# A mixer and FFN kernel: x1 transposed by DMA in f16 halves instead of by TensorE, and 1/den spread over the channels by DMA instead of by a matmul

## The reference, cut to what matters

```python
for _ in range(2):                       # two levels of analysis filters (4 taps, every second token)
    h = dwconv(low, g_filter)[:, ::2]; low = dwconv(low, h_filter)[:, ::2]
q = elu(h16) + 1.0                       # h16: low in 16 heads of 32 channels; k = q, v = h16
kv = einsum('bnhd,bnhe->bhde', q, v);  z = q.sum(axis=1)
num = einsum('bnhd,bhde->bnhe', q, kv)
den = einsum('bnhd,bhd->bnh', q, z)[..., None] + 1e-6
low = num / den
for h in reversed(highs):                # two levels of synthesis filters on doubled tokens
    low = dwconv(repeat(low, 2), h_synth) + dwconv(repeat(h, 2), g_synth)
x1 = _layernorm(x + layer_norm(x + low, gamma, beta))
out = _layernorm(x1 + (silu(x1 @ wg.T) * (x1 @ wu.T)) @ wd.T)
```

## Time and profile before

| | us |
|---|---|
| median of three runs | 1384.56 |
| profiled execution, span from first to last instruction | 1382.5 |
| median above the span | 2.1 |
| TensorE busy | 1245.5 (90%) |
| VectorE busy | 988.1 (71%) |
| ScalarE busy | 688.8 (50%) |
| GpSimd busy | 373.0 (27%) |
| iterations 1 to 8, from first `gate_up` to first `gate_up` | 155.6, 154.1, 154.4, 148.0, 144.4, 144.4, 144.3, 127.6 |

### The profile page before, as it was taken

How to read it: one execution, slowest core, us unless ns; L and a number is a source line. 1 busy time by engine, 2 the same in 40 slices (tenths; PEclk the granted TensorE clock), 3 DMA queues, 4 the chain that set the end, 5 groups by cost and what they waited for, 6 DMA issues and landing times.

```text
span 1382.5 us, 18903 instructions
## 1 busy us (share of the span) xinstructions
PE 1245.5 (90%) x5920; PEld 629.5 (46%) x5920; DVE 988.1 (71%) x1913; ACT 688.8 (50%) x1384; POOL 373.0 (27%) x790
## 2 busy tenths in 40 slices
PE   3997039998999989998999999999999999999998
PEld 3885025444444444444544444444444444444443
DVE  2677938988688958988489738883898478854332
ACT  2663046345753466346753466346634664365432
POOL 2001033133423044223413143304321341234101
PEclk9998559999999999999999999999999999999999
DMA  8963033000520014000500041002200130010000
GB/s 262 285 238 123 0 123 108 23 24 24 176 77 31 0 55 147 20 23 24 176 16 31 8 148 30 31 1 84 100 23 8 53 122 23 15 38 24 16 16 31
DMA packets 48465, 95.20 MB, mean 69 GB/s; under 512 B 8448, under 2 KB 25088, under 8 KB 47376
## 3 DMA queue, kind: packets, MB, share of 16 engines
q1 hardware_dynamic: 48400, 94.42, 20.8%
HBM read 69.21 MB, written 25.19 MB: 68 GB/s over the span
## 4 chain that ended last, share of the span: by engine, by line
DVE 29%; PE 27%; issue 22%; ACT 12%; POOL 9%; SPq 0%; DMA 0%; DVEq 0%; POOLq 0%; ACTq 0%
DVE s_chan L864 6%; DVE h_f L1070 5%; DVE low L864 5%; PE ps_down L540 3%; PE ps_down L539 3%; PE ps_gate L522 3%; PE ps_gate L523 3%; PE ps_up L523 3%; PE ps_up L522 3%; DVE hid L1076 3%; POOL rs L819 3%; DVE h_mem L864 3%; PE ps_down L572 2%; ACT junk L671 2%; DVE l L864 2%
## 5 line engine op out<-in xcount | busy, mean ns | idle before, releaser
L522 PE MATMUL ps_gate<-x_hi,w 128*128 128x512 f16 x768 | 292.4, 381 | 27.5 <-DVE h_f L1070 25.4
L539 PE MATMUL ps_down<-w,hid 128*128 128x512 f16 x768 | 292.1, 380 | 0.1
L540 PE MATMUL ps_down<-w,hid 128*128 128x512 f16 x768 | 292.1, 380 | 0.0
L523 PE MATMUL ps_gate<-x_lo,w 128*128 128x512 f16 x768 | 292.0, 380 | 0.0
L522 PE MATMUL ps_up<-x_hi,w 128*128 128x512 f16 x768 | 291.1, 379 | 0.0
L523 PE MATMUL ps_up<-x_lo,w 128*128 128x512 f16 x768 | 291.1, 379 | 0.0
L758 ACT ACTIVATE hid<-h_f 128x512 f16<-128x512 f32 x192 | 121.0, 630 | 203.2 <-DVE h_f L1070 203.2
L1070 DVE SCALAR_TENSOR_TENSOR h_f<-ps_up,gate_s 128x512 f32<-128x512 f32 x192 | 131.7, 686 | 123.7 <-ACT gate_s L754 123.1
L1076 DVE TENSOR_TENSOR hid<-h_f,hid 128x512 f16<-128x512 f32 x192 | 139.3, 725 | 57.7 <-ACT hid L758 56.8
L754 ACT ACTIVATE gate_s<-ps_gate 128x512 f32<-128x512 f32 x192 | 112.1, 584 | 70.0 <-PE ps_up L523 69.8
L522 PEld LDWEIGHTS ps_gate<-x_hi,w 128*128 128x128 f16 x768 | 75.2, 98 | 124.9 <-DVE h_f L1070 42.2
(11 more groups left out here) (106 smaller groups left out, 1803.8 us busy)
## 6 DMA issues: line engine op xcount, KB each, us to landing
xa<-x_chan SPq DMA_DIRECT2D x32, 515.0 KB, 5.6
xb<-x_chan SPq DMA_DIRECT2D x8, 2060.0 KB, 8.9
xt<-x_tok SPq DMA_DIRECT2D x64, 256.0 KB, 2.6
out<-z SPq DMA_DIRECT2D x64, 256.0 KB, 2.0
hid<-weights SPq DMA_DIRECT2D x12, 768.0 KB, 6.7
q_in<-q_scratch SPq DMA_DIRECT2D x8, 518.0 KB, 8.5
h_in<-h_scratch SPq DMA_DIRECT2D x8, 518.0 KB, 9.5
h_scratch<-h SPq DMA_DIRECT2D x8, 512.0 KB, 9.2
```

The source lines that it names most:

```text
L522: pe.matmul(ps_gu[k % 2][g][:, :], w, x1_hi[:, b, c, :], start=(c == 0), stop=False)
L523: mm = pe.matmul(ps_gu[k % 2][g][:, :], w, x1_lo[:, b, c, :], start=False, stop=(c == NC - 1))
L539: pe.matmul(ps_d[t % 2][:, :], h_hi[:, k, t * P:(t + 1) * P], w, start=(k == 0), stop=False)
L540: mm = pe.matmul(ps_d[t % 2][:, :], h_lo[:, k, t * P:(t + 1) * P], w, start=False, stop=(k == NH - 1))
```

## The change

x1 is split in token layout. ScalarE writes the f16 high half from the same inputs as x1 just before x1 itself (one more pass in `normx`), GpSimd subtracts it from x1 for the low half (a new `normx` there), and SyncE transposes both halves by DMA, two DMAs per tile (`norm3` on SyncE). The halves of a tile lie in the tile's own buffer of `xt` (`x1_tok`), so `xt` is loaded again only after both transposes have landed (`reload`). TensorE's `norm3`, ScalarE's copy and VectorE's subtraction are gone. The first `gate_up` of a block waits for eight landings.

The sums of den go to four groups of 32 columns, one per 128 channels, each a matmul of its own; den then has 128 partitions, 4 useful ones in each group of 32. SyncE stores 1/den to DRAM, waits for that, and loads it four times, each row repeated over the 32 channels of its head, straight into `att`, which now has four buffers. The spreading matmul and its copy are gone.

```diff
@@ BESIDE: block 0 of an iteration, then block 1 @@
-    (0, 4): [(LATE, "kv", 0), (LATE, "blocks", 0), (NOW, "norm3", 4), (NOW, "xbeta", 7), (NEXT, "high1", 0)],
+    (0, 4): [(LATE, "kv", 0), (LATE, "blocks", 0), (NOW, "norm3", 5), (NOW, "reload", 4), (NOW, "xbeta", 6),
+             (NEXT, "high1", 0)],
...
-    (1, 13): [(NEXT, "norm3", 0), (NEXT, "normx", 2), (NEXT, "norm2", 3), (NEXT, "normq", 3)],
-    (1, 14): [(NEXT, "norm3", 1), (NEXT, "normx", 3)],
-    (1, 15): [(NEXT, "norm3", 2)],
-    (1, 15.5): [(NEXT, "norm3", 3), (ANA, "exp", 0)],
+    (1, 13): [(NEXT, "norm3", 1), (NEXT, "reload", 0), (NEXT, "normx", 2), (NEXT, "norm2", 3), (NEXT, "normq", 3)],
+    (1, 14): [(NEXT, "norm3", 2), (NEXT, "reload", 1), (NEXT, "normx", 3)],
+    (1, 15): [(NEXT, "reload", 2), (NEXT, "norm3", 3), (NEXT, "reload", 3)],
+    (1, 15.5): [(ANA, "exp", 0)],
...
+    den_dram = nc.dram_tensor("den_scratch", [P, QW], F32, kind="Internal").ap()
...
-        z_heads = sb("z_heads", [P, NC, HEADS])
-        den = sb("den", [HEADS, QW])
-        att = sb("att", [P, 2, QW])
+        z_heads = sb("z_heads", [P, NC, HEAD])
+        den = sb("den", [P, QW])
+        att = sb("att", [P, NC, QW])
+        x1_tok = xt[:, :, :].rearrange("p t c -> p (t c)").bitcast(F16).rearrange("p (t w c) -> p t w c", t=4, w=2)
...
@@ SyncE @@
-            def after_norm2(j, batch, t):
+            def norm3(j, batch, t):
+                b, u = t // DSUB, t % DSUB
+                if not first(j):
+                    hold(sp, gu_ready, NH * (2 * j + b - 1))
+                for w, (x1_part, ready) in enumerate(((x1_hi, x1_hi_ready), (x1_lo, x1_lo_ready))):
+                    hold(sp, ready, SUBS * j + t + 1)
+                    sp.dma_start_transpose(x1_part[:, b, :, u * P:(u + 1) * P], x1_tok[:, u, w, :]
+                                           ).then_inc(x1_turned[w][u], 16)
+
+            def reload(j, batch, t):
...
-                hold(sp, r_ready, SUBS * j + t + 1)
+                for w in range(2):
+                    hold(sp, x1_turned[w][t % DSUB], 16 * (2 * j + t // DSUB + 1))
                 load_xt(j + (t + 4) // SUBS, (t + 4) % SUBS)
+
+            def dens(j, batch, _):
+                hold(sp, den_step, 2 * (j + 1))
+                sp.dma_start(den_dram[:, :], den[:, :]).then_inc(st_den, 16)
+                hold(sp, st_den, 16 * (j + 1))
+                for c in range(NC):
+                    rows = den_dram[c * HEAD:c * HEAD + CHUNK_HEADS, :]
+                    sp.dma_start(att[:, c, :], rows[:, None, :].to_broadcast([CHUNK_HEADS, HEAD, QW])
+                                 ).then_inc(ld_att[c], 16)
...
@@ TensorE @@
             def dens(j, batch, _):
...
-                    mm = pe.matmul(ps_y[0:HEADS, 0:QW], z_heads[:, c, :], q_in[:, c, :], start=(c == 0),
-                                   stop=(c == NC - 1))
+                    mm = pe.matmul(ps_y[c * HEAD:(c + 1) * HEAD, 0:QW], z_heads[:, c, :], q_in[:, c, :],
+                                   start=True, stop=True)
...
             def attend(j, batch, c):
...
-                pe.matmul(ps_y[:, 0:QW], spread[:, c, :], den[:, :], start=True, stop=True)
                 pe.matmul(ps_x[:, 0:QW], kv_blocks[:, c, :], q_in[:, c, :], start=True, stop=True
                           ).then_inc(qk_ready, 1)
...
-            def norm3(j, batch, t):
...
-                for c in range(NC):
-                    mm = pe.transpose(ps_y[:, c * P:(c + 1) * P], x1[:, t, c * P:(c + 1) * P], ident[:, :])
-                mm.then_inc(x1_turned, 1)
...
             def gate_up(B, b, k):
                 if k == 0:
-                    pe.wait_ge(x1_hi_ready, DSUB * (B + 1))
-                    pe.wait_ge(x1_lo_ready, DSUB * (B + 1))
+                    for u in range(DSUB):
+                        pe.wait_ge(x1_turned[0][u], 16 * (B + 1))
+                        pe.wait_ge(x1_turned[1][u], 16 * (B + 1))
...
@@ ScalarE @@
-            def attend(j, batch, c):
...
-                nc.scalar.activation(att[:, c % 2, :], ps_y[:, 0:QW], ACT.Copy).then_inc(rden_out, 1)
...
             def normx(j, batch, t):
...
+                nc.scalar.activation(x1_tok[:, t % DSUB, 0, :], x1[:, t, :], ACT.Identity, bias=rs2[:, t, 5:6],
+                                     scale=rs2[:, t, 4:5]).then_inc(x1_hi_ready, 1)
                 nc.scalar.activation(x1[:, t, :], x1[:, t, :], ACT.Identity, bias=rs2[:, t, 5:6],
                                      scale=rs2[:, t, 4:5]).then_inc(x1_ready, 1)
-            def norm3(j, batch, t):
...
@@ GpSimd @@
+            def normx(j, batch, t):
+                n = SUBS * j + t + 1
+                pool.wait_ge(x1_ready, n)
+                pool.wait_ge(x1_hi_ready, n)
+                nc.gpsimd.tensor_tensor(x1_tok[:, t % DSUB, 1, :], x1[:, t, :], x1_tok[:, t % DSUB, 0, :],
+                                        ALU.subtract).then_inc(x1_lo_ready, 1)
...
@@ VectorE @@
             def attend(j, batch, c):
-                dve.wait_ge(rden_out, NC * j + c + 1)
-                V.tensor_tensor(att[:, c % 2, :], ps_x[:, 0:QW], att[:, c % 2, :], ALU.mult).then_inc(att_done, 1)
+                dve.wait_ge(qk_ready, NC * j + c + 1)
+                dve.wait_ge(ld_att[c], 16 * (j + 1))
+                V.tensor_tensor(att[:, c, :], ps_x[:, 0:QW], att[:, c, :], ALU.mult).then_inc(att_done, 1)
...
-            def norm3(j, batch, t):
...
-                V.tensor_tensor(x1_lo[:, t // DSUB, :, cols], ps_y[:, :].rearrange("p (c n) -> p c n", c=NC),
-                                x1_hi[:, t // DSUB, :, cols], ALU.subtract).then_inc(x1_lo_ready, 1)
```

More of the change, by code:

```diff
@@ L117 @@
 for _s in range(DSUB + 3):
-    FIRST_NORM += [(name, _s - lag) for name, lag in (("norm2", 0), ("normq", 0), ("normx", 1), ("norm3", 3))
+    FIRST_NORM += [(name, _s - lag) for name, lag in (("norm2", 0), ("normq", 0), ("normx", 1), ("norm3", 1), ("reload", 1))
                    if 0 <= _s - lag < DSUB]
@@ L374, in next_bands @@
                 load_bands(j, batch)
-            steps = {"low1": low1, "keys": keys_store, "norm2": after_norm2, "bands": next_bands}
+            steps = {"low1": low1, "keys": keys_store, "norm3": norm3, "reload": reload, "dens": dens,
+                     "bands": next_bands}
             run = before(steps)
@@ L779, in _ @@
             pool.wait_ge(set_pool, 2)
-            pool.wait_ge(ld_const, 128)
+            pool.wait_ge(ld_const, 112)
             for n in range(16):
@@ L825, in normq @@
                                 var2, rstd2, shift2)
-            steps = {"norm1": norm1, "norm1q": norm1q, "xbeta": xbeta, "norm2": norm2, "normq": normq}
+            steps = {"norm1": norm1, "norm1q": norm1q, "xbeta": xbeta, "norm2": norm2, "normq": normq,
+                    "normx": normx}
             before(steps)(FIRST_NORM, 0, 0)
@@ L934, in dens @@
                 dve.wait_ge(den_ready, j + 1)
-                V.tensor_scalar(den[:, :], ps_y[0:HEADS, 0:QW], ATTN_EPS, None, ALU.add).then_inc(den_step, 1)
+                if not first(j):
+                    dve.wait_ge(st_den, 16 * j)
+                V.tensor_scalar(den[:, :], ps_y[:, 0:QW], ATTN_EPS, None, ALU.add).then_inc(den_step, 1)
                 dve.wait_ge(den_step, 2 * j + 1)
```

84 lines of the change are left out of this document (28 added, 56 removed).

## The result

The changed kernel takes 1491.98 us (median of 4 runs, 1491.14 to 1493.0) beside 1384.38 us before (4 runs): the ratio is 1.078, 95% interval 1.0765 to 1.0795, 7.8% slower. The forecast was 1464 us, 5.8% slower, with a range of 1395 to 1545. The profiled execution has a span of 1490.4 us; TensorE's mean granted clock is 0.926 of full speed, 0.971 before.

A forecast was written before the change was run, and what follows sets the result against it. TensorE is busy for 90% of the span, and at an iteration's end the ScalarE and GpSimd chain arrives with it, without slack. 1382.5 + 7 x (9.1 + 1.6) + 5 = 1462.4 us, plus 2.1 around it: 1464; range 1395 to 1545.

The forecast's parts named there:

- the walk: End of an iteration, trace times stepped through ScalarE, GpSimd and SyncE in the changed order: next iteration 9.1 us later.
- The gates at the end: Next iteration's first gate_up: tile 3's last half lands at 968.5 us against 959.2 before, start 9.1 us later.
- the other gate: SyncE's queue at an iteration's end: tile 3's transposes wait behind output tile 2's store, whose normalisation ends at 964.4 us.
- The landing: Transposing DMA of a tile's half, 128 KB: taken as 2.6 us, like a 256 KB load; bounds 2.0 to 9.2.
- Rival 1: Transposes at iteration ends are slow: tile 3's pair needs 9.2 us instead of 2.6, total 1510 or 1556; chance 0.2.
- Rival 2: Norm chain at iteration ends closes up: half the delay taken back, 4.5 us per boundary, total 1421 us; chance 0.18.
- The clock: First gate_up after a pause of 12 us: TensorE at half clock costs 1.6 us, seven times; bounds 0 and 1.6.
- Upstream: Iteration start to 925 us: TensorE's relief against delayed silu and h_f, sum 0, between -4 and +4 us per iteration.
- den's sums: Four den matmuls at position 8: gain taken as 0; if the four run at once, 1.4 us per iteration go.
- The opening: Before the first gate_up: it comes 4 us later, 1/den's round trip adds 1; together +5 us.
- rival 3: TensorE is the bound; pairs land before its block ends at 955.8, iterations shorten by 7.8 us, total 1335; chance 0.09.
- The signs: Profile after: gate_up idle 80 to 90 us in seven pauses, PEclk 0.5 behind, subtraction 1.3 to 1.4 us, squares waiting longer.

The follow-up runs named there:

- The plain copies: Changed kernel with each transposing DMA replaced by a plain DMA of the same bytes, transposition left out: 1479.21 us, ratio 1.0692.
- fillers: Changed kernel with 40, then 57 extra unneeded matmuls on TensorE before each iteration's first gate_up: 1489.33 us, then 1485.31 us.
- Den's part alone: Kernel before with only four column tiles for den and 1/den by DMA, x1 as before: 1383.62 us, ratio 0.9998.
- the subtraction moved: Changed kernel with GpSimd's subtraction placed behind the next tile's mean and scales: 1462.68 us, ratio 1.0568.
- half by DMA: Kernel before with den's part, only tiles 4 to 7 transposed by DMA, their subtraction behind the next tile's mean and scales: 1387.17 us, ratio 1.002.
- beta earlier: Kernel with tiles 4 to 7 by DMA, GpSimd's beta additions moved to where no VectorE filter step runs: 1380.75 us, ratio 0.9976.

## Why the prediction was right, and where its sizes were off

The direction and the place were right: TensorE loses 32 f32 spreads and 64 tiles of transposes, gains nothing, and waits at the end of each iteration for the last x_lo. The size was less right. With its own bounds upstream, 7 times -4 to +4, the walk allows 1436 to 1492 us, so that the 1492 measured is at its upper end, and the last link of the walk was not the one that the trace shows. Step by step:

- **The gates at the end.** Predicted 9.1 us later, measured 11.1. Counted from the norm of tile 0, the walk through ScalarE and GpSimd held: output tile 2 normalised after 38.5 us (measured 37.7), TensorE's block ended after 29.9 (measured 33.7, with a wait for z and the slow step behind it). From that normalisation to the next gate_up the walk had 4.1 us, and it took 6.9. The mis-sized term is the issue on SyncE: a transposing DMA was put at the 0.35 us of a plain one, and it is 1.2. With six of them behind the store of output tile 0, the queue is the last link, and ScalarE no longer: the store of tile 2 did not wait (its data were there at 1023.5, the issue was at 1024.7). The plain copies show the other gate, which the prediction had named, right behind it.
- **The landing.** Taken as 2.6 us; measured 2.5 from the start of the issue at the median, and 2.8 to 3.8 for the x_lo that ends the pause. Rival 1, slow transposes at 9.2 us, is out. The Trainium skill has 1309 ns for a 128x128 block ("VectorE: DVE Perf Modes", The three transpose paths); four such blocks one after the other, 5.2 us by the estimate in the prediction, is not how a half lands, which is there in 2.5 us.
- **The chain.** Rival 2, the chain closing up, is out: the walk's 38.5 us to the normalisation of output tile 2 came out as 37.7, and no pause of the changed kernel is under 10.3 us.
- **The clock.** Predicted 1.6 us once per iteration, seven times. The first eight matmuls behind the seven pauses took 3.2 to 3.4 us instead of 1.73, and the fillers show it as time of the iteration. But the slow step also came after the waits at position 9 of block 0 and position 15 of block 1, of 2.67 and 2.27 us. In the fifth iteration with 40 fillers both were absent, and the waits behind them were longer by as much, 1.5 and 1.7 us: those two cost nothing.
- **Upstream.** Predicted 0, between -4 and +4; measured +4.9, of which 1.5 is the clock's at the boundary and 3.4 the rest, within the bounds. The subtraction ahead of the next mean cost some 4 us per iteration over all (29 us in the total). This is the largest miss of the sum: 4.3 us of relief were set against that delay. Den's part alone gave back 0.3 us in a plain iteration, and with the subtraction moved TensorE's block, without the clock's part, is 142.4 us against 144.2: of the 4.3 us some 2 came back at best, and in the changed kernel they were outweighed.
- **den's sums.** I took 0; the Trainium skill's rule ("TensorEngine Tiling (Array Packing)", Theoretical Speedup) gave up to 1.4 us per iteration. The group went from 1.93 to 0.64 us, a factor of 3.0, so the rule holds for the matmuls, and 0 is right for the time.
- **The opening** +4.3 (predicted +5). **The last iteration** +3.8 (predicted 0): it has block 0's stalls too, which I had left out of the count by speaking only of its missing successor.
- **TensorE as the bound** (rival 3) is out. In the kernel with half by DMA there is no pause at the boundary, and a plain iteration still takes 145.2 us against 144.4; with beta earlier it is 143.8, a small part of what TensorE was relieved of.
- **The signs.** The pauses sum to 81 us (80 to 90 foretold), each with the clock at 0.5 behind it, and the squares of x1 wait 107.6 us for GpSimd's mean instead of 72.6. The subtraction takes 1.25 us at the mean (1.3 to 1.4 foretold). For the loads of 1/den VectorE waits once, 6.8 us at the opening, and in no iteration.

The sum with the measured sizes, against the profiled span: 1382.5 + 4.3 + 103.6 = 1490.4 us, the span after. That is a division of the measured difference and no proof of it. In the same way the end of the iteration (11.1), the clock behind it (1.5) and the rest upstream (3.4) are the 16.0 us of a plain one.

Open: why the first three iterations, beside which the analysis runs, lose only 11.4 to 13.4 us where the plain ones lose 16. Their pauses are no shorter (11.9 to 12.7 us). It is TensorE's block that differs: without the clock's part it is 1.0 to 1.3 us shorter than before in them, and 3.7 to 3.8 longer in the plain ones. What makes that difference was not looked into. Open too is whether issuing the stores and the reloads from another engine's queue, so that SyncE's holds only the transposes, would pay; that was not tried.
